# A fourth key group for VectorE's transposes, and a new order of work around them, in a three-block perceiver kernel

## What is computed

```python
h = layernorm(x)
x = x + softmax((h @ Wq + bq) @ (ctx @ Wk + bk).T / sqrt(512)) @ (ctx @ Wv + bv)
h = layernorm(x); n = layernorm(h) * ln_w + ln_b       # per batch, 16 heads of 32
q, k, v = l2norm(n @ Wq2), l2norm(n @ Wk2), h @ Wv2
x = x + ((sigmoid((q @ k.T - 0.29514) * 15) * gate_q * gate_k) @ v) @ Wo + bo
e = argmax(layernorm(x) @ gate_w.T)                    # one expert of 8 a row
x = x + expert_e(sigmoid(max logit) * layernorm(x))
```

## Time and profile before

| | us |
|---|---|
| median of 3 runs | 384.33 |
| lowest, highest | 381.88, 384.96 |
| the profiled execution | 382.74 |
| its span, first to last instruction | 380.6 |
| mean granted TensorE clock | 0.964 of full |

### The profile page before, as it was taken

How to read it: one execution, slowest core, us unless ns; L and a number is a source line. 1 busy time by engine, 2 the same in 40 slices (tenths; PEclk the granted TensorE clock), 3 DMA queues, 4 the chain that set the end, 5 groups by cost and what they waited for, 6 DMA issues and landing times.

```text
span 380.6 us, 5836 instructions
## 1 busy us (share of the span) xinstructions
PE 343.1 (90%) x2154; PEld 214.9 (56%) x2154; DVE 161.4 (42%) x357; ACT 93.9 (25%) x215; POOL 81.9 (22%) x87
## 2 busy tenths in 40 slices
PE   1999189999999989999998999999889988799993
PEld 1777056853546644455653455643436778788781
DVE  4126018423253755280757254332463644255322
ACT  1232012135113481111663112242313300000000
POOL 4000007332024200223400210332023302512122
PEclk9999759879999999999999999999999999899998
DMA  7999999928999205999301997100891142910000
GB/s 265 268 185 334 365 386 219 183 61 297 384 197 184 51 0 193 370 293 187 62 0 53 344 372 296 43 0 2 339 420 67 50 175 102 342 68 19 30 25 26
DMA packets 48613, 69.05 MB, mean 181 GB/s; under 512 B 2598, under 2 KB 27206, under 8 KB 47568
## 3 DMA queue, kind: packets, MB, share of 16 engines
q1 hardware_dynamic: 46592, 62.94, 59.0%
q0 software_dynamic: 2000, 5.83, 4.1%
HBM read 65.61 MB, written 4.19 MB: 183 GB/s over the span
## 4 chain that ended last, share of the span: by engine, by line
PE 66%; SPq 10%; issue 6%; DMA 6%; DVE 4%; ACT 4%; POOL 3%; DVEq 0%; ACTq 0%; POOLq 0%
PE ST L1071 12%; PE A L975 11%; PE SC L1046 9%; PE A L1254 8%; PE TR L970 7%; SPq L298 6%; DMA AW_sb<-awk 4%; PE TR L975 4%; PE SC L1236 3%; PE A L970 2%; PE A L1017 2%; SPq L285 2%; SPq L288 1%; SPq L309 1%; PE SC L1211 1%
## 5 line engine op out<-in xcount | busy, mean ns | idle before, releaser
L1071 PE MATMUL ST<-CTX_sb,PR_sb 128*64 128x512 f32 (+1 forms) x208 | 47.7, 599 | 2.2 <-ACT PR_sb L276 2.2
L970 PE MATMUL TR<-ident_sb,CTX_sb 128*128 128x128 f32 (+1 forms) x224 | 31.0, 282 | 11.0 <-DMA CTX_sb<-ctx 10.1
L970 PEld LDWEIGHTS TR<-ident_sb,CTX_sb 128*128 128x128 f32 (+1 forms) x224 | 24.9, 147 | 22.2 <-DMA CTX_sb<-ctx 10.9
L688 DVE STREAM_TRANSPOSE CT_sb<-FF_sb 128x1024 f32<-128x1024 f32 x24 | 28.3, 1218 | 14.6 <-DMA FF_sb<-ctx 13.9
L269 DVE COPY CT_sb<-TR 128x512 f32<-128x512 f32 (+1 forms) x28 | 18.3, 654 | 30.1 <-PE TR L970 26.2
L1071 PEld LDWEIGHTS ST<-CTX_sb,PR_sb 128*64 128x64 f32 (+1 forms) x208 | 14.1, 136 | 25.4 <-issue 22.2
L269 ACT COPY CT_sb<-TR 128x512 f32<-128x512 f32 (+1 forms) x28 | 15.5, 553 | 48.4 <-PE TR L970 48.3
L1046 PE MATMUL SC<-CT_sb,qcurP_sb 128*64 128x256 f32 x192 | 26.9, 404 | 0.0
L1046 PE MATMUL SC<-CT_sb,qcur_sb 128*64 128x256 f32 x192 | 25.3, 389 | 0.0
L975 PE MATMUL A<-AW_sb,normT_sb 128*128 128x512 f32 x48 | 22.0, 600 | 0.0
L423 POOL TENSOR_TENSOR rn_sb<-ss_sb,nhalf_sb 128x16 f32<-128x16 f32 x4 | 11.6, 2907 | 39.7 <-DVE ss_sb L762 39.7
(11 more groups left out here) (243 smaller groups left out, 525.7 us busy)
## 6 DMA issues: line engine op xcount, KB each, us to landing
CTX_sb<-ctx SPq DMA_DIRECT2D x24, 1024.0 KB, 9.3
FF_sb<-ctx SPq DMA_DIRECT2D x32, 256.0 KB, 8.8
FF_sb<-ctx SPq DMA_DIRECT2D x32, 128.0 KB, 5.9
CTX_sb<-wgu SPq DMA_DIRECT2D x4, 1024.0 KB, 9.1
CTX_sb<-wdn SPq DMA_DIRECT2D x5, 512.0 KB, 11.1
FF_sb<-wgu SPq DMA_DIRECT2D x2, 1024.0 KB, 6.2
rows<-XR_sb SPq DMA_DIRECT2D x3, 512.0 KB, 10.2
CTX_sb<-ctx SPq DMA_DIRECT2D x8, 130.0 KB
```

The source lines that it names most:

```text
L688: v.transpose(ctxT[:, grp % 2, k, :, :].rearrange("p c (b r) -> p b c r", r=Q), split[:, k, n * BLOCKS:(n + 1) * BLOCKS, :].rearrange("p b ...
L970: last = t_.transpose(bank[:, c * w:c * w + n], rows[:, c * P:(c + 1) * P], ident[0:n, 0:n])
L1071: last = t_.matmul(ST[q, :], probs[0:w, t, q], ctxb[0:w, k, t, :], start=(t == 0), stop=(t == KT - 1))
```

## The change

Pairs 1 to 3 have groups 0, 1, 3 and 5 turned by DVE; PE turns 2, 4 and 6, in the order 0, 1, 2, 3, 5, 4, 6. Group 5's copy takes the slot in `FF` that group 0 leaves, so SP loads it (`last_split`) when the pair's group 0 has been turned, behind the previous loads in its queue. DVE turns it at u = 6, ahead of that half-step's attention work. Pair 0 has its own order, 2, 4, 5, 6, 0, 1, 3, with DVE turning 0, 1 and 3; SP loads chunks 1, 2, 3 ahead of the split copies there, and chunk 0 and wv behind awq and awk. Its tiles 4 and 5 are turned ahead of the wide brings. The gate sums move to u = 10 to 13, two each, behind the turns. The next queries move from ahead of the exponentials into the sums, half at c = 0 and half at c = 3, and the next pair's groups 0 and 1 are both turned at c = 1, behind the normalisation steps. The split copies of the next pair are waited for in the order group 3, then groups 0 and 1 once the last turn is done. Semaphore counts follow.

```diff
-SPLIT_GROUPS = (0, 1, 3)
-SPLIT_LOADS = ((0, 2), (2, 3))
-TURNED_TILES = [t for t in range(KT) if t // GT not in SPLIT_GROUPS]
+SLOT_OF = {0: 0, 1: 1, 3: 2, 5: 0}
+SPLIT_PARTS = ((0, 1), (3,), (5,))
+EARLY = 2
+TURN_FIRST = 6
...
+class Order:
+    def __init__(self, groups, split):
+        self.groups = groups
+        self.split = [g for g in groups if g in split]
+        self.at = {g: i for i, g in enumerate(groups)}
+        self.tiles = [t for g in groups if g not in split for t in range(g * GT, min(g * GT + GT, KT))]
+        last = sorted((max(self.at[t // GT] for t in range(lo, hi)), c) for c, (lo, hi) in enumerate(CHUNKS))
+        self.ready = {c: at + 1 for at, c in last}
+        self.maxima = [c for _, c in last]
+        self.max_at = {2 * at + 3: c for at, c in last if 2 * at + 3 < 2 * GROUPS}
+    def tile(self, u):
+        pos = u // GT + 1
+        t = self.groups[pos] * GT + u % GT if pos < GROUPS else KT
+        return t if t in self.tiles else None
+    def split_at(self, u):
+        pos = u // GT + 1
+        return self.groups[pos] if u % GT == 0 and pos < GROUPS and self.groups[pos] in self.split else None
+FIRST = Order((2, 4, 5, 6, 0, 1, 3), (0, 1, 3))
+NEXT = Order((0, 1, 2, 3, 5, 4, 6), (0, 1, 3, 5))
...
-MAX_AT = {5: 0, 9: 1, 13: 2}
-KEY_MOVES = len(TURNED_TILES)
-MOVES = KEY_MOVES + NCH // 2
+NUM_MOVES = NCH // 2
...
+        def slot_free(eng, p, pos):
+            earlier(eng, "scored", GROUPS * p + (pos - 1 if pos else 0))
...
+            def next_split(p):
+                sp.wait_ge(s["keysT_made"], split_turned(p, order_of(p).split.index(3) + 1))
+                settle(sp)
+                load_split(p + 1, 1)
+                sp.wait_ge(s["keysT_made"], split_turned(p, len(order_of(p).split)))
+                settle(sp)
+                load_split(p + 1, 0)
...
-            load_split(0)
-            load_pair(0, (1, 2, 3, 0))
-            load_weight(wv, "wv", "wv_in")
+            load_pair(0, (1, 2, 3))
+            load_split(0, 0)
+            load_split(0, 1)
             sp.wait_ge(s["qp_made"], 2 * DC)
             load_weight(awq, "awq", "aq_in")
             load_weight(awk, "awk", "ak_in")
+            load_pair(0, (0,))
+            load_weight(wv, "wv", "wv_in")
             load_weight(awv, "awv", "av_in")
-            load_split(1)
+            next_split(0)
...
+            def last_split(p):
+                sp.wait_ge(s["keysT_made"], split_turned(p, 1))
+                settle(sp)
+                load_split(p, 2)
             with sp.Fori(1, PAIRS - 1) as p:
+                last_split(p)
                 load_x(p)
-                load_split(p + 1)
+                next_split(p)
                 load_pair(p + 1)
                 store_rows(p - 1)
+            last_split(PAIRS - 1)
             load_x(PAIRS - 1)
-            sp.wait_ge(s["keysT_made"], 2 * len(SPLIT_GROUPS) * PAIRS)
+            sp.wait_ge(s["keysT_made"], split_turned(PAIRS, 0))
...
-            next_queries(1)
+            next_queries(1, FIRST.at[FIRST.split[-1]] + 1)
             def pair(p, by_scores, by_max, by_sums):
                 for u in range(2 * GROUPS):
                     for step in by_scores.get(u, ()):
                         attention(p - 1, step)
-                    move_keys(act, a.copy, p, 0, GT + u)
-                if not is_last(p):
-                    next_queries(p + 1)
+                    move_keys(act, a.copy, p, 0, NEXT.tile(u))
                 exponentials(p)
                 for step in by_max:
                     attention(p - 1, step)
                 move_numerators(act, a.copy, p, 0)
                 for c in range(NCH):
+                    if c in (0, 3) and not is_last(p):
+                        next_queries(p + 1, NEXT.at[NEXT.split[-1]] + 1, (0, 1) if c == 0 else (2, 3))
...
-            turn_split(0, 0)
-            turn_split(0, 1)
             first_queries()
+            for t in FIRST.tiles[:GT]:
+                move_keys(dve, v.tensor_copy, 0, 1, t)
             for u in range(2 * GROUPS):
-                if u in MAX_AT:
-                    maximum(0, MAX_AT[u])
-                if u % 2 == 0 and u >= GT:
-                    turn_split(0, u // 2 + 1)
-                move_keys(dve, v.tensor_copy, 0, 1, GT + u)
-                n = u - (2 * GROUPS - 1 - 2 * DC)
-                if 0 <= n < 2 * DC:
-                    dve.wait_ge(s["gmul"], n + 1)
-                    at = HEADS * (n // DC)
-                    v.tensor_reduce(wgate[:, n % DC, at:at + HEADS], (sq, kh)[n % 2][:, :].rearrange("p (h d) -> p h d", h=HEADS),
-                                    AX.X, ALU.add).then_inc(s["gred"], 1)
+                if u in FIRST.max_at:
+                    maximum(0, FIRST.max_at[u])
+                turn_split(0, FIRST.split_at(u))
+                move_keys(dve, v.tensor_copy, 0, 1, FIRST.tile(u))
+                for n in range(2 * (u - (2 * GROUPS - DC)), 2 * (u - (2 * GROUPS - DC)) + 2):
+                    if n >= 0:
+                        dve.wait_ge(s["gmul"], n + 1)
+                        at = HEADS * (n // DC)
+                        v.tensor_reduce(wgate[:, n % DC, at:at + HEADS], (sq, kh)[n % 2][:, :].rearrange("p (h d) -> p h d", h=HEADS),
+                                        AX.X, ALU.add).then_inc(s["gred"], 1)
             shift(0)
             for c in range(1, NCH, 2):
                 move_numerators(dve, v.tensor_copy, 0, c)
-                turn_split(1, c // 2)
+                turn_split(1, NEXT.groups[c // 2])
             def pair(p, by_scores, by_max, by_sums):
                 for u in range(2 * GROUPS):
+                    if u == TURN_FIRST:
+                        turn_split(p, NEXT.split_at(u))
                     for step in by_scores.get(u, ()):
                         attention(p - 1, step)
-                    if u in MAX_AT:
-                        maximum(p, MAX_AT[u])
-                    if u % 2 == 0 and u >= GT:
-                        turn_split(p, u // 2 + 1)
-                    move_keys(dve, v.tensor_copy, p, 1, GT + u)
+                    if u in NEXT.max_at:
+                        maximum(p, NEXT.max_at[u])
+                    if u // GT + 1 >= EARLY and u != TURN_FIRST:
+                        turn_split(p, NEXT.split_at(u))
+                    move_keys(dve, v.tensor_copy, p, 1, NEXT.tile(u))
                 shift(p)
                 for step in by_max:
                     attention(p - 1, step)
@@ -883,8 +953,9 @@
                         move_numerators(dve, v.tensor_copy, p, c + 1)
                     for step in by_sums.get(c, ()):
                         attention(p - 1, step)
-                    if c < 2 and not is_last(p):
-                        turn_split(p + 1, c)
+                    if c == 1 and not is_last(p):
+                        for grp in NEXT.groups[:EARLY]:
+                            turn_split(p + 1, grp)
...
-                first = isinstance(p, int) and p == 0
-                if first:
+                o = order_of(p)
+                if is_first(p):
+                    for t in o.tiles[:GT]:
+                        turn_keys(p, t)
                     bring(False, 0)
                     bring(False, 1)
                 for u in range(2 * GROUPS):
                     for step in by_scores.get(u, ()):
                         attention(p - 1, step)
-                    turn_keys(p, GT + u)
+                    turn_keys(p, o.tile(u))
```

110 lines of the change are left out of this document (64 added, 46 removed).

## The result

The changed kernel takes 370.86 us in the median (370.14 to 375.19, 4 runs) against 383.58 (381.88 to 384.96, 4 runs) beside it. The ratio is 0.9706, with a 95% interval of 0.9661 to 0.9751: faster by 2.9%. Its profiled execution took 370.14, with a span of 368.4 where that of before was 380.6, so 12.2 us are to be accounted for; 14.6 had been forecast.

A forecast was written before the change was run, and what follows sets the result against it. TensorE, busy nine tenths of the span, was taken as the bound. Gains of 8.0 (start) + 2x(1.35+0.95) (pairs 1 and 2) + 2.0 (pair 3) = 14.6 us led to 369 us, range 365.5 to 376.

The forecast's parts named there:

- A, as summed: Whole kernel: the summed gains arrive as forecast, time 367.5 to 371; chance 0.58.
- The start: First pair up to its weighting: last score near 62.0 instead of 70.16, weighting near 75.5; gain taken as 8.0 us.
- The cover of the gate chain: First pair: bias matmuls and half-clock brings end at 74.4, hiding the gate chain (exponentials over at 72.7) by 1.7 us.
- rival B: First pair: brings at full clock, so the gate chain is no longer hidden; 9.1 us gained there, time 368; chance 0.10.
- Pair 1: First looped pair: 2.3 us shorter, 1.35 from group 5 leaving PE and 0.95 from moving the next queries.
- D: Steady pairs give only low bounds, or group 5's copy holds DVE 1 us each; 3.7 less gain, 373.4; chance 0.06.
- F: Pairs 1 to 3: group 5's copy lands so late that DVE and attention stand; slower than before, 388; chance 0.02.
- Pair 2: Second looped pair: 2.3 us shorter, 1.35 from group 5 (bounds 0.7 and 2.04) and 0.95 from the queries.
- Pair 3: Last pair, with no next queries and a wider attention chain: 2.0 us gained from group 5 leaving PE.
- The normalisation ahead of the turns: Weighting of a pair with a next one: worth 0 by itself, up to 1 us a pair if left out.
- The clock: First pair on PE: granted clock 1.00 from 28 to 66; 0.50 before 66 would show the forecast wrong.
- rival E: First pair's scores: clock 1.2 GHz instead of 2.4 from 41 to 52; 9 us less gain, 378.5; chance 0.04.

The follow-up runs named there:

- e1: The changed kernel with group 5's copy issued between chunks 1 and 2 of its pair's loads; 369.84 us, ratio 0.970 against before.
- e4: The changed kernel with the next queries back in one piece ahead of the exponentials; 373.55 us, ratio 0.978 against before.
- e7: The changed kernel with the next pair's groups 0 and 1 turned at c = 0 and 1, ahead of the normalisation; 371.35 us, ratio 0.969 against before.
- e3: The changed kernel with only groups 0, 1 and 3 turned by DVE in pairs 1 to 3, plain order; 373.27 us, ratio 0.978 against before.
- e9: The kernel before, with only the wait for chunk 0 ahead of tile 4 dropped; 384.31 us, ratio 1.009.
- e10: The kernel before, with only the gate sums moved to u = 10 to 13, behind the turns; 380.06 us, ratio 0.998.
- e11: The kernel before, with the wait for chunk 0 dropped and the gate sums moved to u = 10 to 13; 374.71 us, ratio 0.978.
- v1: e1 with pair 1's split copies of groups 0 and 1 issued sooner and awo behind group 5's copy; 368.15 us, ratio 0.964 against before.
- e5: The changed kernel with pair 0's old order of groups and loads, gate sums still behind the turns; 372.68 us, ratio 0.974 against before.
- e6: The changed kernel with the gate sums back at u = 5 to 12, one each; 371.98 us, ratio 0.976 against before.
- v2: v1 with bias matmuls in TensorE's waits for turns, gate products and sums 2 to 7 later, awo ahead of group 5's copy; 367.16 us, ratio 0.957 against before.
- v3: v2 with pair 1's loads reordered: chunk 1 first, then group 5's copy and awo, then chunks 0, 2, 3; 361.40 us, ratio 0.945 against before.

## Why the prediction was right, and where it was not

The forecast was 369 in a range of 365.5 to 376; the time is 370.86. Its likeliest case was *A, as summed*, 367.5 to 371. By the steps:

- **The start: 8.0 forecast, 7.92 measured.** The forward schedule held row by row: last first-pair score 62.0 forecast, 62.26 measured; TensorE's waits for the turns 1.8 forecast for the first, 2.08 measured; turns at 52 to 60, 52.39 to 60.26 measured; first weighting 75.5, measured 75.64. The agreement to 0.1 us is in part luck. The same pair 0 started pair 1 at 85.5 in e1, e4 and e7 and at 87.51 in e3, so this execution lies at the long end of what the code does.
- **Its cause was read wrong.** I took TensorE's idle stretch at 39.3 to 47.8 for keys loaded late and credited the new order of loads. It was a wait for chunk 0, of which TensorE turns nothing (the weighting, which does need it, has a wait of its own), and it hid a second one, for awk. The prediction names awk, but not that the two lie side by side. e9, e10 and e11 show that removing both in the kernel before gives 7.5 of the 7.9 us, with no load moved. The sum was right since it was built on when data is there and an engine free, and did not depend on what had been in the way. It also took for granted, without saying so, that the old wait is gone: in after chunk 0 is issued only at 40.96 and is there 12.3 to 13.8 us later, and with the old condition tile 4, turned at 32.92, would have waited for it. Anyone who had asked me which part of the change to keep would have got a wrong answer.
- **The cover of the gate chain** held as said: with the brings at 1.2 GHz the weighting follows them (75.64). The case of full clock, rival B, came up in e3 and v1: behind the same bias matmuls the brings take 5.41 us, TensorE waits 1.5 for the exponentials, and the weighting starts at 73.45 and 73.64 (74.4 forecast). But the clock falls in the weighting, so 8.4 and 8.2 us are gained at the start and not 9.1. The largest gain, 10.4, is in e1, e4 and e7, where the brings take 7.10 and the clock is back for the weighting at 73.1 to 73.2; in e7 it is lost again in pair 1 (63.11). TensorE in e3:

```profile
65.23 5.41 PE L1087 MATMUL A<-AO_sb,WQK_sb 128*128 128x384 f32 x16
```

- **Pair 1: 2.3 forecast, 0.63 measured. This is the step that failed**, by 1.7 of the 2.4 us between 14.6 and 12.2; most of the others is the longer rest. The term was group 5's copy, "about 105" with slack 1; it was turned at 108.32. Issue began at 91.84, as I had it (91.2), but 8 issues took 9.73 us, and behind them the pieces moved at the slow rate. The late turn holds the sum of q's squares to 110.61, and so both powers, `gates` (118.99) and the copies behind it, and TensorE waits 1.86 at 120.49. The mechanism is that of rivals D and F, in one pair of three. e3 prices it: group 5 is worth -0.2 in pair 1; by e1, with the copy there in time and no wait for chunk 1, pair 1 would take 58.1, which is worked out and not measured.
- **Pair 2: 2.3 forecast, 2.46 measured**: 0.92 for the queries (0.95 forecast; e3 and e4 agree) and 1.54 for group 5 (1.35 forecast, bounds 0.7 and 2.04). **Pair 3: 2.0 forecast, 2.07 measured** (e3).
- **The normalisation ahead of the turns: 0 forecast, up to 1 a pair if left out; measured 0.14** in pair 2 (e7).
- **The rest, from pair 3's weighting on, 0.9 longer.** I had no term for it. The code there is the same in all fourteen kernels, which take 125.5 to 127.9 for it, and before and the three that differ from it only in pair 0 take 125.5 to 126.9. So 0.9 is within what the same code shows. The traces say where it arises: up to the first expert matmul all fourteen take 72.4 to 72.6. Behind it before, after and five others run their first block of expert matmuls at low clock (2.98 to 3.68 us for 16 matmuls), e1, e4, e5 and e11 wait 0.9 to 2.0 for VectorE, and e6, e9 and e10, the three shortest, do neither (2.05). Why an execution falls into one case or another stays open. TensorE in after and in before:

```profile
313.12 3.31 PE L1331 MATMUL A<-QK_sb,FF_sb 128*128 128x128 f32 x16 [0.78 <-DVE QK_sb L1005]
326.14 3.46 PE L1254 MATMUL A<-QK_sb,FF_sb 128*128 128x128 f32 x16 [0.78 <-DVE QK_sb L934]
```

- **The clock**: I had it at 1.00 from 28 to 66. It was 1.00 in 40 to 60, waits of up to 2.08 us included, so rival E did not come. Then it was 0.95 in 60 to 65 and 0.50 in 65 to 70, a little sooner than said. The rule of the Trainium skill (TensorE: Matmul & The Clock Gate, PE-mode transpose), that transposes don't count as busy for the clock, had made E likelier. The trace of after kept 1.00 with transposes and scores in turn; no stretch of it has transposes alone, so it does not test the rule by itself.

## What to carry to other kernels

A wait in the trace is named by what ended it last; before putting its end down to "late data", look up in the code which semaphores the instruction waits for, and whether it uses what they stand for. Two waits that run side by side hide each other: dropping one can give nothing, or cost a little, and only dropping both pays, so a null result of one edit says nothing on the pair. When the start of a pipeline is pulled forward by 8 us, ask of every later load when it is issued and what stands ahead of it in the queue: here v2 gave back in pair 1 5.6 of the 7.8 us that its start had gained, and v3 took half of that back by issuing first what is wanted first.
